# Adding y in step 1 of the last segments, and maxima of a block ahead of the wait for the last denominators

## The chip, the cores and the metric

The kernel runs on one core of a Trainium2 chip. The metric is the device time of one execution in microseconds (us). Five engines work side by side, each through its own program in order: TensorE (PE; its weight loads are listed apart as PEld), VectorE (DVE), ScalarE (ACT), GpSimd (POOL) and SyncE (SP, which here only issues DMAs). They wait for each other by semaphores.

## The reference

x is 2048 rows by 256, the context 1601 rows by 256. The reference is

- x = x + tanh(g_xattn) * (attention(layernorm(x), context) @ Wo + bo). The attention layer normalises its two inputs once more, has 16 heads of 64, clips the scaled scores to -11 and 11, and divides by the sum of the exponentials: softmax(clip(q k^T / 8)) v.
- x = x + tanh(g_ffn) * ffn(layernorm(x)). The feed-forward part (256 to 768 and back) has weights rounded to 4 bits in blocks of 32, and activations rounded to 16 bits by a scale of the whole tensor: `scale = max|x| / 32767`, so that no element of a stage can be rounded before the maximum of all of them is known. There are five such scales, one after the other.

Everything is float32.

## The kernel before

**Segments.** The attention runs over 32 segments (`SEGS`). A segment is a pair of heads and a block of 512 rows of x (`ORDER`): pair t // 4 and block t % 4 for t up to 23, then pairs 6 and 7, three blocks each, and in segments 30 and 31 block 3 of both. A segment has 13 steps (`ST`), each over 128 rows of the context. In a step

- TensorE computes the scores of two steps ahead (`scores`, L1080) into PSUM,
- ScalarE takes the exponential into `e_buf` (L509), and with that frees the scores' banks,
- VectorE clips it between exp(-11) and exp(11) (L793) and adds it to `acc`, the running sum for the denominators (`add_e`, L749), one step behind the clip,
- TensorE multiplies the clipped exponentials by the values (`values`, L1096).

**Jobs.** Two more PSUM banks (`ps_m`) are used in turn by jobs, whose order `segment_jobs` writes out for each segment; a job's number modulo 2 is its bank, and it waits (`bank_free`) until the job two before it has been taken out of the bank. TensorE does the jobs of a segment in step 0 (`at == st`), after the scores of step 2 and before the values of step 0. In their order they are: key and value projections for a later pair (`k`, `v`; only in the segments for which `kv_blocks` is not empty, 0 to 26), the next segment's q (L990), two halves of y for each segment in `y_segments` (L1039: the finished heads' output times Wo), the denominators of the segment or segments before (`den_job`, L1018: ones times `acc`), and in segments 27 to 29 three jobs that transpose quantised feed-forward weights (`wT`, L979). In segments 27 to 31 there is thus: q, 2 y, den, 3 wT in 27 and 29; q, 4 y, den, 3 wT in 28; q, 2 y, den in 30; and 2 y, den in 31.

ScalarE takes q out (L443), the denominators (`den_take`, L483) and the high parts of the transposed weights (L476), all after the exponential of step 2. VectorE takes y out: `add_y` (L785) adds a half of it to `xacc`. With `w_low` (L730) it takes the low parts of the weights. So in a segment without projections the chain in the two banks is: q is taken by ScalarE, then y half 1 can be written; y half 0 is taken by VectorE, then the denominators can be; y half 1 is taken, then the first `wT`; and so on.

**VectorE's order** is written out in its `run` (L788 to L822). In step 0 it clips and makes the last addition of the segment before; in step 1 it clips and joins the two halves of the segment before's output (`join_out`, L776); from step 2 on it clips and adds. In step 2 it then calls `add_y` for the segments that are due. In segments 29 to 31 `norm_piece` puts the layer norm for the feed-forward part in between: moments, small operations of a Newton iteration (`root_step`), and in segment 31 the maxima of the normalised rows of blocks 0 and 1 (`h_tops`, steps 1 and 2). ScalarE writes those rows (`h_normalise`, L488): eight after the exponential of step 0 of segment 31, four after that of step 12.

**The turn of the denominators.** SP moves them from one row to many partitions, VectorE inverts them in step 6 (L763), SP brings them back, and `scale_out` (L770) multiplies the output by them in step 11.

**The end of attention** (L824 to L852). TensorE multiplies segment 30's output by Wo (`y_last`, L1051), writes the denominators of segment 31 (`den_last`, L1027), waits for VectorE and multiplies the output of 31. VectorE joins the output halves, waits for the denominators, takes the maxima of block 2 (`h_tops(NBS - 2)`), inverts the denominators in two halves (L835), multiplies (L841), adds y (L846), and makes the layer norm of block 3. Behind it the first global scale is formed, the rows become integers, and the feed-forward matmuls begin (L1189).

Of the kernel before, what the change touches and what calls it, by code (L numbers as in the profile page):

```python
# [22 lines left out]
NBS = N // NB  # L23
# [58 lines left out]
def kv_blocks(t):  # L82

    if t < SEGS - 2 * NBS:
        return [(t // NBS + 1, t % NBS)] if t else [(1, 0)]
    return {WT0 - 3: [(PAIRS - 1, 0)], WT0 - 2: [(PAIRS - 1, 1)], WT0 - 1: [(PAIRS - 1, 2), (PAIRS - 1, 3)]}.get(t, [])
# [7 lines left out]
def turn_in(t):  # L94

    return next((i for i, segs in enumerate(DENS) if segs[-1] == t - 1), None)
# [6 lines left out]
def y_segments(t):  # L103

    if t <= WT0:
        return [t - 3] if t >= 3 else []
    return [t - 3, t - 2] if t == WT0 + 1 else [t - 2]
# [35 lines left out]
def bank_of(key):  # L143
    return JOBS[key] % 2


def place_of(key, seg):

    return JOBS[key] // 2


def attention_ffn(nc, x, ctx_rows, g_xattn, g_ffn, ln_l_w, ln_l_b, ln_c_w, ln_c_b,
                  Wq, Wkv, Wo, bo, w_gate, w_up, w_down, out):
    inv_rows = nc.dram_tensor("inv_rows", (4, NB), F32).ap()
    with ExitStack() as ctx:
# [102 lines left out]
        def await_job(eng, key, seg=None):  # L258

            eng.wait_ge(job_ready[bank_of(key)], place_of(key, seg) + 1)  # L260
# [339 lines left out]
        def _(dve):  # L600
# [40 lines left out]
            def top(dst, src):  # L641
                return dve.tensor_reduce(dst, src, AX_X, ALU.max, apply_absolute_value=True)  # L642
# [27 lines left out]
            def h_tops(b):  # L670

                dve.wait_ge(h_norm, 4 * b + 4)
                top(fst[:, 0, 2 * b:2 * b + 2],
                    z[:, 4 * b:4 * b + 4, :].rearrange("p (a t) d -> p a (t d)", a=2)).then_inc(h_top, 1)

            def norm_piece(t0, st, place):

                if (t0, st, place) in ((SEGS - 3, 4, 1), (SEGS - 2, 4, 1), (SEGS - 1, 3, 1)):
                    b = t0 - (SEGS - 3)
                    for half in range(2):  # L680
                        await_taken(dve, ("y", t0 - 2, half))
                    moments(LN3 + 4 * b, rows_of_block(b))
                k = 2 * (st - 5) + place
                if t0 == SEGS - 2 and 0 <= k <= 3 + 3 * NEWTON:
                    root_step(LN3, LN3 + 2 * NBS, k)
                k += 2
                if t0 == SEGS - 1 and 0 <= k <= 3 + 3 * NEWTON:
                    root_step(LN3 + 2 * NBS, LN3 + 3 * NBS, k)
                if t0 == SEGS - 1 and place == 1 and st in (1, 2):
                    h_tops(st - 1)  # L690
# [23 lines left out]
            def w_scales(w):  # L714

                blocks = wpiece[w].rearrange("p (n e) -> p n e", e=QB)
                dve.wait_ge(in_w, 64)
                link(top(wsc[:, w, 0, :], blocks))
                link(dve.tensor_scalar(wsc[:, w, 1, :], wsc[:, w, 0, :], 1.0 / WMAX, 1e-12, ALU.mult, ALU.max))
                dve.reciprocal(wsc[:, w, 2, :], wsc[:, w, 1, :]).then_inc(w_inverse, 1)  # L720

            def w_integers(w):
                dve.wait_ge(w_scaled, w + 1)
                dve.tensor_scalar(wpiece[w], wpiece[w], MAGIC, MAGIC, ALU.add, ALU.subtract).then_inc(w_round, 1)
# [8 lines left out]
            def w_multiply(w, row, ready, done):  # L733

                blocks = wpiece[w].rearrange("p (n e) -> p n e", e=QB)
                dve.wait_ge(ready, w + 1)
                dve.tensor_tensor(blocks, blocks, wsc[:, w, row, :].unsqueeze(2).to_broadcast([P, WBLK, QB]),
                                  ALU.mult).then_inc(done, 1)

            def add_e(seg, st):  # L740

                t0, r = seg.t0, rows_of(st)
                if st == 1:
                    a = e_buf[:, (ST * t0) % E_BUFS, :, :]
                else:
                    a = acc[0:r, t0 % 3, :, :]
                    dve.wait_ge(summed, seg.count(ST - 1, st - 1))
                dve.wait_ge(clip_done, seg.count(ST, st + 1))
                dve.tensor_tensor(acc[0:r, t0 % 3, :, :], a, e_buf[0:r, (ST * t0 + st) % E_BUFS, :, :],  # L749
                                  ALU.add).then_inc(summed, 1)  # L750

            def add_bias(b):

                dve.wait_ge(bias_scaled, 1)
                dve.wait_ge(lat_pool, NT - 4)
                rows = xacc[:, 4 * b:4 * b + 4, :]
                dve.tensor_tensor(rows, rows, bo_t[:, :].unsqueeze(1).to_broadcast([P, 4, DM]), ALU.add).then_inc(bias_added, 1)

            def invert_spread(i):

                dve.wait_ge(den_landed, 16 * rows_turned(i + 1))
                rows = 2 * QB * len(DENS[i])
                dve.reciprocal(inv_spread[0:rows, :], den_spread[0:rows, :]).then_inc(inv_done, 1)  # L763

            def scale_out(seg, t):

                i = turn_of(t)
                dve.wait_ge(inv_landed, 16 * rows_turned(i + 1))
                dve.wait_ge(o_out, Seg(t).count(1, 1))
                dve.tensor_tensor(oT[:, t % 3, :], oT[:, t % 3, :], rden[:, DENS[i].index(t), :], ALU.mult).then_inc(norm_done, 1)  # L770

            def join_out(seg, t):

                s = Seg(t)
                dve.wait_ge(o_half, s.count(1, 1))
                dve.tensor_tensor(oT[:, t % 3, :], ps_o[:, 1, :], oT[:, t % 3, :], ALU.add).then_inc(o_out, 1)  # L776

            def add_y(seg, t, half):
                key = ("y", t, half)
                n0 = 4 * ORDER[t][1] + 2 * half  # L780
                await_job(dve, key, seg)
                if t < NBS:
                    dve.wait_ge(bias_added, NBS)
                dst = xacc[:, n0:n0 + 2, :]
                dve.tensor_tensor(dst, ps_m[:, bank_of(key), :].rearrange("p (t d) -> p t d", d=DM), dst,  # L785
                                  ALU.add).then_inc(job_taken[bank_of(key)], 1)

            def run(seg):  # L788
                t0 = seg.t0
                for st in range(ST):  # L790
                    dve.wait_ge(exp_done, seg.count(ST, st + 1))
                    tile = e_buf[:, (ST * t0 + st) % E_BUFS, :, :]
                    dve.tensor_scalar(tile, tile, EXP_LO, EXP_HI, ALU.max, ALU.min).then_inc(clip_done, 1)  # L793
                    norm_piece(t0, st, 0)
                    if st >= 2:
                        add_e(seg, st - 1)
                    elif st == 0 and t0 >= 1:
                        add_e(Seg(t0 - 1), ST - 1)
                    elif t0 >= 1:
                        join_out(seg, t0 - 1)  # L800
                    if t0 == 0 and 4 <= st < 4 + NBS:
                        add_bias(st - 4)
                    if st == 6 and turn_in(t0) is not None:
                        invert_spread(turn_in(t0))
                    if st == 11 and turn_in(t0) is not None:
                        for t in DENS[turn_in(t0)]:
                            scale_out(seg, t)
                    if st == 2 and WQ0 <= t0 < WQ0 + 12 and (t0 - WQ0) % 2 == 0:
                        w = (t0 - WQ0) // 2
                        w_scales(w)  # L810
                        w_multiply(w, 2, w_inverse, w_scaled)
                    if st == 2:
                        for t in y_segments(t0):
                            add_y(seg, t, 0)
                            add_y(seg, t, 1)
                    if st == 2 and WQ0 <= t0 < WQ0 + 12 and (t0 - WQ0) % 2 == 0:
                        w_integers(w)
                        w_multiply(w, 1, w_round, w_quant)
                    if st == 2 and WT0 <= t0 < WT0 + 3:
                        for j in range(3):  # L820
                            w_low(t0 - WT0, j)
                    norm_piece(t0, st, 1)  # L822

            segments(dve, run)  # L824
            end = Seg(SEGS)
            t = SEGS - 1
            add_e(Seg(t), ST - 1)
            join_out(end, t)
            den_bank, w = bank_of(("den", t)), NB // 2
            await_job(dve, ("den", t))  # L830
            dve.wait_ge(o_out, SEGS)
            h_tops(NBS - 2)
            for half in range(2):
                part = slice(w * half, w * half + w)
                ins = dve.reciprocal(rden[:, 0, part], ps_m[:, den_bank, part])  # L835
# [440 lines left out]
```

## Time and profile before

| | us |
|---|---|
| median of 3 runs | 1190.52 |
| lowest and highest run | 1189.46, 1191.87 |
| the profiled execution | 1192.05 |
| its span, first to last instruction | 1190.1 |
| TensorE busy | 1094.1 |
| VectorE busy | 974.3 |
| ScalarE busy | 621.2 |

The profile is of one execution. The attention takes its first 1011 us, with some 29 us for each segment, the feed-forward part the rest. In the order of time, what stands in brackets is how long the engine was idle before the instruction, and whose work it then waited for. Matmuls of float32 are recorded in more than one piece, and neighbouring records overlap, because the ends of matmuls are modelled. [...]

### The profile page before, as it was taken

The page shows a single profiled execution, that of the slowest core. Times are in us where ns is not written, and L with a number is a line of the kernel's source. Part 1 is how long each engine was busy: PE and PEld are TensorE (multiplying, and loading weights), DVE is VectorE, ACT ScalarE, POOL GpSimd, SP SyncE. Part 2 cuts the span into 40 slices and gives each one's busy share as a digit, 9 for nine tenths or more (in the row PEclk, how much of TensorE's full clock was granted, in tenths as well). Part 3 has the DMA queues.
Part 4 walks back from the last instruction along what each step waited for, and adds up shares of the span by engine and source line. Part 5 has one row for each costly group of instructions (what it writes and reads, how often), then busy time and mean ns, then how long its engine had stood idle before and what let it go on. Part 6 is the DMA issues. An engine that isn't in the chain of part 4 may idle for free.

```text
span 1190.1 us, 20382 instructions
## 1 busy us (share of the span) xinstructions
PE 1094.1 (92%) x8424; PEld 497.5 (42%) x8424; DVE 974.3 (82%) x1319; ACT 621.2 (52%) x719; POOL 29.5 (2%) x41
## 2 busy tenths in 40 slices
PE   3999999999999999999999999999999989699039
PEld 2443344434443444344434443444333322587039
DVE  7467978797879788988898889887888898849986
ACT  2455555555555555555555555555555554449652
POOL 1200000000000000000000000000000000003200
PEclk9999999999999999999999999999999999799559
DMA  5000300010001000100010001000000000000002
GB/s 166 1 1 2 116 1 20 1 37 2 20 1 37 1 19 2 36 1 20 1 37 2 19 1 37 1 19 1 19 10 11 10 10 10 1 1 1 0 1 72
DMA packets 27324, 22.23 MB, mean 19 GB/s; under 512 B 8478, under 2 KB 23007, under 8 KB 27231
## 3 DMA queue, kind: packets, MB, share of 16 engines
q1 hardware_dynamic: 27230, 20.92, 5.8%
q8 instruction: 67, 1.10, 0.4%
q14 instruction: 27, 0.21, 0.1%
HBM read 18.55 MB, written 2.22 MB: 17 GB/s over the span
## 4 chain that ended last, share of the span: by engine, by line
PE 77%; DVE 12%; ACT 5%; issue 4%; DMA 1%; SPq 0%; POOL 0%; POOLq 0%; DVEq 0%; ACTq 0%
PE ps L1096 26%; PE ps L1080 26%; PE ps L990 4%; DVE acc L749 4%; PE ps L998 4%; PE ps L1039 4%; PE ps L1007 4%; PE ps L1189 3%; PE ps L1225 3%; DVE e_buf L793 3%; PE ps L1018 2%; ACT e_buf L509 1%; PE ps L979 1%; DVE gt L917 1%; ACT z L579 1%
## 5 line engine op out<-in xcount | busy, mean ns | idle before, releaser
L509 ACT ACTIVATE e_buf<-ps 128x1024 f32<-128x1024 f32 x416 | 426.1, 1025 | 312.3 <-PE ps L1080 312.3
L1096 PE MATMUL ps<-e_buf,vb 64*64 64x512 f32 x3328 | 436.3, 594 | 4.0 <-DVE e_buf L793 3.8
L749 DVE TENSOR_TENSOR acc<-acc,e_buf 128x1024 f32<-128x1024 f32 (+1 forms) x352 | 426.9, 1213 | 0.0
L793 DVE TENSOR_SCALAR e_buf<-e_buf 128x1024 f32<-128x1024 f32 x416 | 283.0, 680 | 108.5 <-ACT e_buf L509 108.3
L1096 PEld LDWEIGHTS ps<-e_buf,vb 64*64 64x64 f32 x3328 | 119.9, 133 | 243.4 <-issue 212.2
L1080 PE MATMUL ps<-qb,kb_even 64*64 64x512 f32 x1664 | 215.9, 589 | 1.3 <-ACT e_buf L509 1.3
L1080 PE MATMUL ps<-qb,kb_odd 64*64 64x512 f32 x1664 | 216.0, 589 | 0.0
L1080 PEld LDWEIGHTS ps<-qb,kb_odd 64*64 64x64 f32 x1664 | 63.8, 133 | 115.3 <-issue 115.3
L1080 PEld LDWEIGHTS ps<-qb,kb_even 64*64 64x64 f32 x1664 | 63.6, 133 | 115.3 <-issue 113.6
L785 DVE TENSOR_TENSOR xacc<-ps,xacc 128x512 f32<-128x512 f32 x60 | 40.9, 688 | 51.8 <-PE ps L1039 51.8
L1189 PE MATMUL ps<-hT,wgu 128*128 128x512 f32 x288 | 70.2, 407 | 2.3 <-DVE hT L886 2.3
L990 PE MATMUL ps<-latT,wst 128*128 128x512 f32 x128 | 63.1, 616 | 2.5 <-ACT latT L437 1.1
L1189 PEld LDWEIGHTS ps<-hT,wgu 128*128 128x128 f32 x288 | 55.9, 195 | 16.0 <-DVE hT L886 2.5
L1039 PE MATMUL ps<-wo_g,oT 128*128 128x256 f32 x240 | 59.1, 389 | 0.3 <-DVE xacc L785 0.3
L642 DVE TENSOR_REDUCE fst<-gt 128x2 f32<-128x1024 f32 x36 | 43.5, 1211 | 18.7 <-ACT gt L564 18.7
L1007 PEld LDWEIGHTS ps<-wst,ctxT 128*128 128x128 f32 (+1 forms) x416 | 49.4, 187 | 11.6 <-issue 11.2
L1039 PEld LDWEIGHTS ps<-wo_g,oT 128*128 128x128 f32 x240 | 43.1, 189 | 24.1 <-issue 14.2
L998 PE MATMUL ps<-ctxT,wst 128*128 128x512 f32 (+1 forms) x128 | 51.9, 532 | 0.0
L1007 PE MATMUL ps<-wst,ctxT 128*128 128x128 f32 (+1 forms) x416 | 51.3, 275 | 0.3 <-ACT vb L454 0.3
L1182 PE MATMUL ps<-ident,fsc 128*128 128x128 f32 x10 | 2.8, 399 | 46.6 <-DVE fsc L642 46.6
L443 ACT COPY qb<-ps 128x512 f32<-128x512 f32 x32 | 18.7, 586 | 44.4 <-PE ps L990 44.4
L749 DVE TENSOR_TENSOR acc<-e_buf 128x1024 f32<-128x1024 f32 x32 | 38.8, 1213 | 0.0
(118 smaller groups left out, 620.1 us busy)
## 6 DMA issues: line engine op xcount, KB each, us to landing
rden<-inv_rows SPq DMA_DIRECT2D x62, 128.0 KB, 2.8
xacc<-in_x_dram SPq DMA_DIRECT2D x4, 512.0 KB, 8.2
wst<-in_L_xattn_Wkv_dram SPq DMA_DIRECT2D x16, 128.0 KB, 2.6
out_dram<-z SPq DMA_DIRECT2D x7, 256.0 KB, 2.2
e_buf<-in_ctx_dram SPq DMA_DIRECT2D x3, 512.0 KB, 4.6
wst<-in_L_xattn_Wq_dram SPq DMA_DIRECT2D x8, 128.0 KB, 2.7
wo_raw<-in_L_xattn_Wo_dram SPq DMA_DIRECT2D x8, 128.0 KB, 3.3
den_spread<-den_row SPq DMA_DIRECT2D x62, 2.0 KB, 1.7
```

Source lines behind the costliest of these rows:

```text
L509: nc.scalar.activation(e_buf[:, g % E_BUFS, :, :], sc[:, g % 2, :, :], ACT.Exp, scale=float(DH) ** -0.5).then_inc(exp_done, 1)
L642: return dve.tensor_reduce(dst, src, AX_X, ALU.max, apply_absolute_value=True)
L749: dve.tensor_tensor(acc[0:r, t0 % 3, :, :], a, e_buf[0:r, (ST * t0 + st) % E_BUFS, :, :], ALU.add).then_inc(summed, 1)
L785: dve.tensor_tensor(dst, ps_m[:, bank_of(key), :].rearrange("p (t d) -> p t d", d=DM), dst, ALU.add).then_inc(job_taken[bank_of(key)], 1)
L793: dve.tensor_scalar(tile, tile, EXP_LO, EXP_HI, ALU.max, ALU.min).then_inc(clip_done, 1)
L990: ins = pe.matmul(bank, wst[:, at[0], 0, k, :], latT[:, k, b * NB:(b + 1) * NB], start=(k == 0), stop=(k == KT - 1))
L998: ins = pe.matmul(bank[:, 0:w], wst[:, at[0], 1, k, :], ctxT[:, k, b * NB:b * NB + w], start=(k == 0), stop=(k == KT - 1))
L1007: ins = pe.matmul(bank[0:r, P * i:P * i + P], ctxT[:, k, P * st:P * st + r], wst[:, at[0], 2, k, :], start=(k == 0), stop=(k == KT - 1))
L1039: ins = pe.matmul(bank[:, DM * m:DM * m + DM], oT[:, t % 3, n0:n0 + P], wo_g[:, p % 2, :], start=True, stop=True)
L1080: ins = pe.matmul(sc[at:at + DH, g % 2, h, :], kb[p % 2][rows, P * st + at:P * st + at + DH], qb[rows, t0 % 2, :], start=True, stop=True)
L1096: ins = pe.matmul(ps_o[DH * h:DH * h + DH, half, :], vb[rows, p % 2, st, DH * h:DH * h + DH], e_buf[rows, g % E_BUFS, h, :], start=(st == ...
L1189: ins = pe.matmul(out_ap, lhs(i), rhs(j), start=(first and n == 0), stop=(last and n == 2))
```

## The change

Two places in VectorE's program. In segments for which `kv_blocks` is empty (27 to 31), `add_y` is called in step 1, behind `join_out` and ahead of what `norm_piece` does there, instead of in step 2; in segments 3 to 26 it stays in step 2. At the end, `h_tops` of block 2 is called before VectorE waits for the last denominators.

```diff
@@ run of VectorE @@
                         w_scales(w)
                         w_multiply(w, 2, w_inverse, w_scaled)
-                    if st == 2:
+                    if st == (2 if kv_blocks(t0) else 1):
                         for t in y_segments(t0):
                             add_y(seg, t, 0)
                             add_y(seg, t, 1)
@@ after the segments @@
             join_out(end, t)
             den_bank, w = bank_of(("den", t)), NB // 2
+            h_tops(NBS - 2)
             await_job(dve, ("den", t))
             dve.wait_ge(o_out, SEGS)
-            h_tops(NBS - 2)
             for half in range(2):
```

## Rows read from the trace of the kernel before

**Rows 1.** The page, busy time of each engine in us.
```profile
PE 1094.1 (92%) x8424; PEld 497.5 (42%) x8424; DVE 974.3 (82%) x1319; ACT 621.2 (52%) x719; POOL 29.5 (2%) x41
```

**Rows 2.** Order of time, TensorE, segment 27: start, duration (us), engine, line, what.
```profile
852.30 1.97 PE L1039 MATMUL ps<-wo_g,oT 128*128 128x256 f32 x8
...
855.01 1.05 PE L1018 MATMUL ps<-acc,ones 128*32 128x512 f32 x4 [0.74 <-DVE xacc L785]
```

**Rows 3.** Order of time, ScalarE and VectorE, segment 27.
```profile
852.50 0.59 ACT L443 COPY qb<-ps 128x512 f32<-128x512 f32 x1 [0.86 <-PE ps L990]
852.55 0.67 DVE L793 TENSOR_SCALAR e_buf<-e_buf 128x1024 f32<-128x1024 f32 x1
...
853.15 1.21 DVE L749 TENSOR_TENSOR acc<-e_buf 128x1024 f32<-128x1024 f32 x1
854.28 1.27 DVE L785 TENSOR_TENSOR xacc<-ps,xacc 128x512 f32<-128x512 f32 x2
...
857.30 1.51 DVE L730 TENSOR_TENSOR wgu<-ps,wgu 128x512 fp32r<-128x512 f32 x2 [1.75 <-ACT wgu L476]
...
861.77 0.69 DVE L793 TENSOR_SCALAR e_buf<-e_buf 128x1024 f32<-128x1024 f32 x1 [1.65 <-ACT e_buf L509]
```

**Rows 4.** Order of time, TensorE and VectorE, segment 28.
```profile
885.25 2.00 PE L1039 MATMUL ps<-wo_g,oT 128*128 128x256 f32 x8 [0.29 <-DVE xacc L785]
886.42 0.69 DVE L785 TENSOR_TENSOR xacc<-ps,xacc 128x512 f32<-128x512 f32 x1 [0.63 <-PE ps L1039]
...
887.29 0.69 DVE L785 TENSOR_TENSOR xacc<-ps,xacc 128x512 f32<-128x512 f32 x1 [0.17 <-PE ps L1039]
...
889.47 0.69 DVE L730 TENSOR_TENSOR wgu<-ps,wgu 128x512 fp32r<-128x512 f32 x1 [1.49 <-ACT wgu L476]
```

**Rows 5.** Order of time, TensorE, segment 29.
```profile
917.42 1.05 PE L1018 MATMUL ps<-acc,ones 128*32 128x512 f32 x4 [0.28 <-DVE xacc L785]
```

**Rows 6.** Order of time, TensorE and VectorE, segment 30.
```profile
949.52 1.05 PE L1018 MATMUL ps<-acc,ones 128*32 128x512 f32 x4 [0.74 <-DVE xacc L785]
...
953.58 0.69 DVE L793 TENSOR_SCALAR e_buf<-e_buf 128x1024 f32<-128x1024 f32 x1 [3.51 <-ACT e_buf L509]
```

**Rows 7.** Order of time, VectorE, segment 31.
```profile
978.30 1.21 DVE L642 TENSOR_REDUCE fst<-z 128x2 f32<-128x1024 f32 x1
979.43 0.68 DVE L793 TENSOR_SCALAR e_buf<-e_buf 128x1024 f32<-128x1024 f32 x1
...
981.16 1.28 DVE L785 TENSOR_TENSOR xacc<-ps,xacc 128x512 f32<-128x512 f32 x2
982.36 1.21 DVE L642 TENSOR_REDUCE fst<-z 128x2 f32<-128x1024 f32 x1
987.54 0.69 DVE L793 TENSOR_SCALAR e_buf<-e_buf 128x1024 f32<-128x1024 f32 x1 [3.97 <-ACT e_buf L509]
```

**Rows 8.** Order of time, TensorE, segment 31.
```profile
975.37 1.99 PE L1039 MATMUL ps<-wo_g,oT 128*128 128x256 f32 x8
981.90 1.92 PE L1018 MATMUL ps<-acc,ones 128*32 128x512 f32 x4 [4.53 <-DVE xacc L785]
```

**Rows 9.** Stretches: length, busy (x instructions) of PE, PEld, DVE, ACT, POOL, PEclk, DMA.
```profile
981.90:984.90 3.00, 3.00 (x12) 0.73 (x16) 1.67 (x2) 0.58 (x1) 0.00 (x0) 0.50 0.00 0
990.00:1009.00 19.00, 16.68 (x139) 4.51 (x132) 18.90 (x41) 10.50 (x13) 0.00 (x0) 1.00 0.04 15
1030.80:1036.40 5.60, 5.60 (x13) 4.44 (x14) 4.97 (x8) 4.70 (x10) 0.00 (x0) 0.50 0.01 1
1036.50:1042.10 5.60, 5.60 (x26) 4.51 (x25) 2.44 (x2) 2.22 (x5) 0.00 (x0) 1.00 0.01 3
```

**Rows 10.** Order of time, ScalarE and VectorE, end of attention.
```profile
1004.31 2.06 ACT L488 ACTIVATE z<-xacc,lnt 128x256 f32<-128x256 f32 x4
...
1011.48 1.22 DVE L642 TENSOR_REDUCE fst<-z 128x2 f32<-128x1024 f32 x1 [1.14 <-PE ps L1027]
```

**Rows 11.** Order of time, TensorE, last values of segment 31.
```profile
1007.41 1.09 PE L1096 MATMUL ps<-e_buf,vb 64*64 64x512 f32 x8 [1.25 <-DVE e_buf L793]
```

## The prediction

> **What bounds the kernel now.** I read the page first. TensorE is busy for 92% of the span, VectorE for 82% [rows 1]. So a gain has to be time that TensorE spends waiting, or time in which VectorE alone sets the end. Then I read the order of time around the places that the diff touches: step 2 of segments 27 to 31 (the only ones for which `kv_blocks` is empty and `y_segments` is not), and the end of attention. In each of them the denominators' matmuls (L1018) stand in TensorE's program behind the two halves of y (L1039) and need the PSUM bank that VectorE's `add_y` (L785) frees. VectorE comes to `add_y` only after the clip and the addition of step 2, so TensorE stands: 0.74 us in segment 27 [rows 2], 0.28 in 29 and 0.74 in 30 [rows 5, 6]. In 28, which has two segments' y, it waits 0.29 before the second [rows 4]. In segment 31 it waits 4.53 us [rows 8]. At the end VectorE idles 1.14 us for the last denominators and takes the maxima of block 2 only afterwards [rows 10].
>
> **The change, part by part.** No operation is added or removed, and no DMA; only VectorE's order changes. What an operation of VectorE costs is read from one start to the next: a clip 0.60 us (852.55 to 853.15), an addition of e 1.13 (853.15 to 854.28) [rows 3], a half of y 0.60 (981.16 to 982.36 for two) and a maximum over a block 1.13 (978.30 to 979.43) [rows 7]. The queues of SP and GpSimd are moved past nothing: SP sends the denominators on when ScalarE has copied them, which comes earlier with them, and GpSimd's gate product waits for y of a pair long gone.
>
> *Segment 27.* VectorE is free at 852.55, where the clip of step 2 stands [rows 3]. The first half of y starts on TensorE at 852.30 [rows 2]. A half takes 1.17 us until VectorE can add it (885.25 to 886.42 [rows 4]), so `add_y` of half 0 runs from 853.47. Its bank is free 0.74 us after its start (981.16 to 981.90 [rows 7, 8]), at 854.21. TensorE ends both halves at 852.30 + 1.97 = 854.27, so the denominators start at 854.27 instead of 855.01: 0.74 us. The second half waits for ScalarE's copy of q, which comes at 852.50 by ScalarE's own order [rows 3] and doesn't move. Now what is queued behind: `add_y` of half 1 starts at about 854.32, then clip (+0.60), addition (+0.60) and the first `w_low` (+1.13), which is at 856.65. It started at 857.30 before, set by ScalarE; 0.74 us earlier is 856.56. So 0.09 is given back, since the third transposition waits for `w_low`. Net 0.65.
> *Segment 28.* TensorE ends the first y at 885.25 - 0.29 = 884.97 [rows 4] and began it 1.97 earlier, at 883.00. Half 0 is then added from 884.17, and its bank is free at 884.91, before TensorE asks for it. The 0.29 us wait goes, the rest of the chain to the denominators keeps its length (0.28 stays of it), and `w_low` comes 0.14 later than it could: the last add starts at 887.29 - 0.28 = 887.01, plus 2.33 is 889.34, against 889.47 - 0.28 = 889.19 [rows 4]. Net 0.14.
> *Segment 29.* It is built as 27; the wait is only 0.28 [rows 5], and with `w_low` giving back 0.08 the net is 0.20.
> *Segment 30.* No weights are transposed here, so the whole 0.74 stays [rows 6]. VectorE then idled 3.51 us before the clip of step 3, which covers the clip and addition that are now late.
> Sum of 27 to 30: 1.73. They add up, since in each segment the clip of step 3 waits for ScalarE's exponentials, and these for TensorE (1.65 us of idle in 27 [rows 3], 3.51 in 30), and everything behind it keeps its distances.
>
> *Segment 31.* Here y was ready at 975.37 + 1.99 = 977.36 [rows 8], long before VectorE came. The two halves come to 978.30, where the maximum of block 0 now stands, and 978.90, in place of 981.16 and 981.76 [rows 7]. The denominators start 0.74 after the first, at 979.04 instead of 981.90: 2.86 us, which is certain as far as VectorE's order goes. [...] The exponentials then allow the clip at 979.04 + 4.06 = 983.10. VectorE's own list (two halves, maximum of block 0, clip, addition, maximum of block 1, so 978.30 + 0.60 + 0.60 + 1.13 + 0.60 + 1.13 + 1.13) is through at 983.49, and that is the later one. So clip 3 moves from 987.54 to 983.49: 4.05 us, and VectorE's idle time of 3.97 there is used up. From then to the segment's end VectorE is busy for 18.90 of 19 us, while TensorE is for 16.68 [rows 9] and waits for its clips [rows 11], so the 4.05 reach the end. Lower end 2.86, if the clock falls all the same.
> [...]
>
> *The end.* The maxima of block 2 need `h_norm` of 12, given by ScalarE's four rows at 1004.31 + 2.06 = 1006.37 [rows 10], before VectorE joins the output halves. They move to 1011.48 - 1.14 = 1010.34, into the 1.14 us in which VectorE waits. The reciprocal then starts at 1011.48 instead of one maximum later, just as the denominators are ready. Gain 1.14; nothing runs beside VectorE on that path, so all of it counts. A lower bound is 0 if the reciprocal were held by something unseen; I see nothing that could.
>
> **Sum.** 1.73 + 4.05 + 1.14 = 6.92 us. The profiled execution took 1192.05 us (span 1190.1), which gives 1185.1. It is 1.53 above the median of the three runs, 1190.52, and a little above their highest, so I take the sum off the median: 1183.6. About 0.2% (2.4 us) is what a measurement of this kernel tells from no change.
>
> **Rivals.**
> *A. The clock falls in segment 31 all the same.* Then its gain is 2.86, the total 5.7 and the time 1184.8. For it: TensorE stands in that stretch for 1.67 us and then soon waits for VectorE again. Against: the granted clock stayed at 1.00 through the waits of 990 to 1009, 2.32 us in all [rows 9]. Chance 0.14.
> *B. The clock behind the attention is better.* [...] TensorE's wait at 1011 is 1.14 us shorter, and its work of before lies elsewhere in time; the low stretch may be shorter. Up to 2.8 us more: 1180.8 to 1183. Chance 0.14.
> *C. The new wait sets the pace.* In step 1 VectorE stands 0.92 us for half 0 and about 0.25 for half 1 in segments 27 to 30, with the clips behind it. If its idle time afterwards were less than 1.17, this came on top each time: 4 x 1.17 = 4.7, and the 1.73 would be lost, so the total is 5.19 - 4.7 = 0.5 and the time 1190.0. [...] Against it: [rows 3, 6] show 1.75 + 1.65 us of idle time behind it in segment 27 and 3.51 in 30. Chance 0.05.
> *D. Slower.* One mechanism is large enough: the clock at the first gate matmuls (L1189, from 1030.8). [...] For it: the low level starts from idle times that now lie elsewhere. Against: it was back at 1.00 after 5.6 us there, and within 5 us of matmuls in segment 31 [rows 9]. Chance 0.02.
> That the change doesn't do what it says would be that step 1's additions never free TensorE earlier; only if y came late in all five segments, which [rows 2, 4 to 8] exclude. Left for this and for the unforeseen, 1185.3 to 1188: 0.03.
>
> **Numbers.** My forecast, 1183.6, has 0.62. The range goes to 1181.0, which takes in most of B, and to 1187.2: A with the runs' own spread of 1.3 us about the median, and some 1 us of the terms of 27 to 30. Faster by over 0.2% is all but C and D: 0.93; within 0.2%: 0.05; slower: 0.02.
>
> **What would show it.** In the changed profile: L1018 starts right at the end of L1039 in segments 27 to 30 and with at most 1.7 us of idle time in 31; the granted clock is 1.00 all through segment 31; VectorE has no idle time before the clip of step 3 of segment 31; its wait on L1027 is gone; the waits of L785 for L1039 grow by about 4 us. Wrong would be: a 0.50 stretch in segment 31 (A), clips of step 3 without idle time before them in 27 to 30 (C), or a longer L1189 pass (B, D).

## The result, and the profile of the changed kernel

The changed kernel takes 1183.15 us (median of 6 runs, 1181.53 to 1185.2), the kernel before 1190.73 (6 runs): 7.6 us less. The ratio is 0.993, with a 95% interval of 0.992 to 0.9941, so by the ratio 8.3 us less (7.0 to 9.5). The forecast was 1183.6 in a range of 1181.0 to 1187.2. The profiled execution took 1181.53 us, its span 1179.7; that of before 1192.05 and 1190.1.

TensorE's order of time in the changed kernel, segments 27, 28, 30 and 31 and the end of attention (start, duration in us, line, what; in brackets the idle time before it):

```profile
850.51 1.97 PE L1039 MATMUL ps<-wo_g,oT 128*128 128x256 f32 x8
852.41 1.05 PE L1018 MATMUL ps<-acc,ones 128*32 128x512 f32 x4
...
880.55 3.88 PE L1039 MATMUL ps<-wo_g,oT 128*128 128x256 f32 x16
884.36 1.05 PE L1018 MATMUL ps<-acc,ones 128*32 128x512 f32 x4
...
945.83 1.05 PE L1018 MATMUL ps<-acc,ones 128*32 128x512 f32 x4
...
971.68 1.99 PE L1039 MATMUL ps<-wo_g,oT 128*128 128x256 f32 x8
975.35 1.05 PE L1018 MATMUL ps<-acc,ones 128*32 128x512 f32 x4 [1.67 <-DVE xacc L785]
...
1002.60 1.08 PE L1027 MATMUL ps<-acc,ones 128*64 128x512 f32 x4
```

The waits of [rows 2, 4, 5, 6] are gone (in segment 29 the denominators start at 914.40, 1.90 us after y at 912.50, where it was 2.25): in segment 28 the four halves of y are one row of 16 without a gap. The wait of 4.53 us [rows 8] is 1.67. VectorE's order of time, segments 27, 30 and 31 and the end:

```profile
851.58 0.69 DVE L785 TENSOR_TENSOR xacc<-ps,xacc 128x512 f32<-128x512 f32 x1 [0.74 <-PE ps L1039]
852.52 0.69 DVE L785 TENSOR_TENSOR xacc<-ps,xacc 128x512 f32<-128x512 f32 x1 [0.25 <-PE ps L1039]
853.13 0.68 DVE L793 TENSOR_SCALAR e_buf<-e_buf 128x1024 f32<-128x1024 f32 x1
853.73 1.22 DVE L749 TENSOR_TENSOR acc<-e_buf 128x1024 f32<-128x1024 f32 x1
854.86 1.35 DVE L730 TENSOR_TENSOR wgu<-ps,wgu 128x512 fp32r<-128x512 f32 x2
...
859.32 0.69 DVE L793 TENSOR_SCALAR e_buf<-e_buf 128x1024 f32<-128x1024 f32 x1 [1.65 <-ACT e_buf L509]
...
949.88 0.69 DVE L793 TENSOR_SCALAR e_buf<-e_buf 128x1024 f32<-128x1024 f32 x1 [1.52 <-ACT e_buf L509]
...
974.61 1.28 DVE L785 TENSOR_TENSOR xacc<-ps,xacc 128x512 f32<-128x512 f32 x2
975.81 1.21 DVE L642 TENSOR_REDUCE fst<-z 128x2 f32<-128x1024 f32 x1
976.93 0.68 DVE L793 TENSOR_SCALAR e_buf<-e_buf 128x1024 f32<-128x1024 f32 x1
977.53 1.22 DVE L749 TENSOR_TENSOR acc<-e_buf 128x1024 f32<-128x1024 f32 x1
978.66 1.22 DVE L642 TENSOR_REDUCE fst<-z 128x2 f32<-128x1024 f32 x1
979.79 0.69 DVE L793 TENSOR_SCALAR e_buf<-e_buf 128x1024 f32<-128x1024 f32 x1
...
1002.51 1.21 DVE L642 TENSOR_REDUCE fst<-z 128x2 f32<-128x1024 f32 x1
1003.73 1.76 DVE L835 RECIPROCAL rden<-ps 128x256 f32<-128x256 f32 x1
```

The new waits stand in step 1 (0.74 and 0.25 us), and behind them clip, addition and `w_low` (854.86) follow without a break. The clip of step 3 waits for ScalarE 1.65 us in segment 27, as before [rows 3], and 1.52 instead of 3.51 in segment 30 [rows 6]. In segment 31 that idle time (3.97 [rows 7]) is gone. Over all segments VectorE's waits of L785 for L1039 grew from 51.8 to 56.4 us, by the 4 us or so that the prediction named as a sign. At the end the reciprocal follows the maxima directly, 1.13 us after L1027; before it was 1012.62 - 1010.35 = 2.27, by these rows of the kernel before:

```profile
1010.35 1.08 PE L1027 MATMUL ps<-acc,ones 128*64 128x512 f32 x4
1012.62 1.75 DVE L835 RECIPROCAL rden<-ps 128x256 f32<-128x256 f32 x1
```

The stretches of the changed kernel (length, then the busy us of PE, PEld, DVE, ACT and POOL with their number of instructions, the clock granted to TensorE as a share of its full speed, PEclk in [rows 9], the busy share of the DMA engines and what they moved in GB/s) show no low clock from y of segment 31 to the first reciprocal, and the matmuls of L1189 begin again at 0.50, for some 3 us in this execution where it was 5.6 [rows 9].

```profile
972.00:1004.00 32.00, 27.31 (x208) 8.97 (x206) 31.10 (x56) 16.14 (x20) 0.00 (x0) 1.00 0.04 9
1021.90:1024.90 3.00, 2.97 (x7) 2.40 (x8) 3.00 (x5) 2.97 (x6) 0.00 (x0) 0.50 0.01 3
1025.20:1028.20 3.00, 3.00 (x15) 2.41 (x14) 2.75 (x4) 2.30 (x5) 0.00 (x0) 1.00 0.00 0
```

**Where the time went.** The two executions, cut at the same instructions. A row is the distance from its mark to the next.

| from | before | changed | less | forecast |
|---|---|---|---|---|
| start to y of 27 | 852.30 | 850.51 | 1.79 | 0 |
| y of 27 to y of 28 | 30.70 | 30.04 | 0.66 | 0.65 |
| y of 28 to y of 29 | 32.17 | 31.95 | 0.22 | 0.14 |
| y of 29 to y of 30 | 31.64 | 31.43 | 0.21 | 0.20 |
| y of 30 to y of 31 | 28.56 | 27.75 | 0.81 | 0.74 |
| y of 31 to L1027 | 34.98 | 30.92 | 4.06 | 4.05 |
| L1027 to reciprocal | 2.27 | 1.13 | 1.14 | 1.14 |
| reciprocal to L1189 | 18.18 | 18.20 | -0.02 | 0 |
| L1189 to the end | 159.30 | 157.77 | 1.53 | 0 |
| sum | 1190.10 | 1179.70 | 10.40 | 6.92 |

The six rows that the change touches give 7.10 us. The first row can't be the change's, which begins behind it. It and the last vary between executions: the profile of before has a stretch of 0.50 near its start, that of the changed kernel hasn't. A second profile of the changed kernel (below) had one, began y of 27 at 852.28, had the same middle rows within 0.01 us, and a last row of 159.77; its span, 1183.5, is 6.6 under that of before.

### The profile page after: what moved, and what is told of

The parts are those of the page before. It is cut to its first block, busy times and chain, and to the rows that moved or that the text cites. A ratio compares the mean times of both kernels' runs of the same rounds, so it can differ in the third digit from the quotient of the medians.

```text
span 1179.7 us, 20382 instructions
## 1 busy us (share of the span) xinstructions
PE 1088.9 (92%) x8424; PEld 495.7 (42%) x8424; DVE 974.4 (83%) x1319; ACT 621.4 (53%) x719; POOL 29.5 (3%) x41
## 4 chain that ended last, share of the span: by engine, by line
PE 83%; DVE 8%; ACT 4%; issue 4%; DMA 1%; POOL 0%; POOLq 0%; SPq 0%; DVEq 0%; ACTq 0%
PE ps L1096 29%; PE ps L1080 28%; PE ps L990 5%; PE ps L1039 4%; PE ps L998 4%; PE ps L1007 4%; PE ps L1189 3%; PE ps L1225 3%; DVE acc L749 2%; PE ps L1018 1%; DVE gt L917 1%; ACT z L579 1%; ACT z L581 1%; PE ps L979 1%; DVE fst L642 1%
## 5 line engine op out<-in xcount | busy, mean ns | idle before, releaser
L785 DVE TENSOR_TENSOR xacc<-ps,xacc 128x512 f32<-128x512 f32 x60 | 41.4, 691 | 56.4 <-PE ps L1039 56.4
L1189 PE MATMUL ps<-hT,wgu 128*128 128x512 f32 x288 | 69.0, 402 | 2.2 <-DVE hT L886 2.2
L990 PE MATMUL ps<-latT,wst 128*128 128x512 f32 x128 | 61.4, 602 | 2.5 <-ACT latT L437 1.2
L1189 PEld LDWEIGHTS ps<-hT,wgu 128*128 128x128 f32 x288 | 55.0, 192 | 15.7 <-DVE hT L886 2.5
L1039 PE MATMUL ps<-wo_g,oT 128*128 128x256 f32 x240 | 59.1, 390 | 0.0
L1039 PEld LDWEIGHTS ps<-wo_g,oT 128*128 128x128 f32 x240 | 43.0, 189 | 23.8 <-issue 14.2
```

The lines of the kernel that those rows point to most:

```text
L990: ins = pe.matmul(bank, wst[:, at[0], 0, k, :], latT[:, k, b * NB:(b + 1) * NB], start=(k == 0), stop=(k == KT - 1))
L1039: ins = pe.matmul(bank[:, DM * m:DM * m + DM], oT[:, t % 3, n0:n0 + P], wo_g[:, p % 2, :], start=True, stop=True)
L1189: ins = pe.matmul(out_ap, lhs(i), rhs(j), start=(first and n == 0), stop=(last and n == 2))
```

## The experiments

All times are medians; a difference in us is taken from the ratio to the kernel before on the same chip, with its interval. Since the clock matters, the table has also the time at 0.50: twice one less the mean granted clock, times the span, mean of the runs. This counts the clock as either 1.00 or 0.50, and in windows of 1 us over all 14 traces it is one of the two, or between them in the one window where it changes. The mean clock is on record to 0.001, which is 2.4 us of this time in one run, so differences of a few us mean something only over many runs. In each of the 14 traces some 51 us of it lie in one stretch of the feed-forward part (from about 1092 to 1105 us on), the same in all kernels. The kernels before have 72.9 us (beside the two parts apart, the segments and the first run of the maxima), 72.1 (beside y repeated, y behind the maxima and the first runs with matmuls ahead of L1189) and 73.9 (beside the runs marked as again and the matmuls at the end of attention); for the first row there is none.

| kernel | us | less than before | at 0.50 |
|---|---|---|---|
| both parts (the changed kernel) | 1183.15 | 8.3 (7.0 to 9.5) | 65.0 |
| the same, again | 1184.42 | 7.7 (5.7 to 9.9) | 67.4 |
| y in step 1 alone | 1185.94 | 5.8 (4.4 to 7.3) | 68.2 |
| of these, 31 alone | 1188.03 | 4.1 (2.9 to 5.4) | 69.1 |
| of these, 27 to 30 alone | 1189.78 | 2.0 (1.0 to 3.0) | 75.3 |
| the maxima alone | 1188.16 | 3.1 (2.0 to 4.1) | 68.2 |
| the maxima alone, again on another chip | 1188.69 | 3.1 (1.8 to 4.5) | 70.2 |
| before, y repeated in 31 | 1189.74 | 1.7 (0.5 to 3.0) | 70.3 |
| changed, y behind the maxima in 31 | 1184.19 | 6.8 (5.2 to 8.5) | 66.2 |
| before, matmuls added at the end of attention | 1190.67 | 1.3 (-0.1 to 2.7) | 66.8 |
| changed, matmuls added ahead of L1189 | 1182.19 | 9.2 (7.5 to 10.8) | 61.4 |
| changed, matmuls added at both places | 1180.27 | 10.8 (8.9 to 12.9) | 55.2 |
| the same, again on another chip | 1182.49 | 9.2 (6.9 to 11.4) | 59.8 |

### The two parts apart

Only the first hunk:

```diff
-                    if st == 2:
+                    if st == (2 if kv_blocks(t0) else 1):
```

> The kernel before with only the first part: y added in step 1 of segments 27 to 31. My theory (the parts are separate and each is a shortened wait): 7.58 us measured for the whole less 1.14 of the other part, so 6.0 to 6.5 us under the kernel before, with the maxima of block 2 again 1.14 us behind VectorE's wait for L1027. Rival (a fifth to a quarter of the gain comes from the clock behind the attention, rival B of the prediction, set off by the shorter wait at the end): more than 1.14 is lost, 2 us or more.

Measured: 1185.94 us, ratio 0.9951 (0.9939 to 0.9963), 5.8 us less (4.4 to 7.3). That is a little under the 6.0 to 6.5 expected, and the interval takes in both this and the rival's loss of 2 us or more, so it doesn't decide between them. The distances of segments 27 to 30 in its trace are those of the changed kernel. The trace showed something else at the end of segment 31, on TensorE:

```profile
997.12 1.09 PE L1096 MATMUL ps<-e_buf,vb 64*64 64x512 f32 x8 [0.72 <-DVE e_buf L793]
999.45 1.59 PE L1096 MATMUL ps<-e_buf,vb 64*64 64x512 f32 x8 [1.25 <-DVE e_buf L793]
1000.97 3.14 PE L1051 MATMUL ps<-wo_g,oT 128*128 128x256 f32 x8
```

The stretch of the same kernel behind them (the clock is the 0.53):

```profile
1000.50:1003.50 3.00, 3.00 (x10) 2.07 (x7) 1.87 (x3) 0.59 (x1) 0.00 (x0) 0.53 0.00 0
```

All 14 traces have these two waits ([rows 11] has the second). This time the clock fell after them: 32.56 us from y of 31 to L1027 instead of 30.92. It happened in 2 of the 7 traces in which the denominators of segment 31 had found it at 1.00 (this one and the one with matmuls ahead of L1189, 32.57 us).

Only the second hunk:

```diff
+            h_tops(NBS - 2)
             await_job(dve, ("den", t))
             dve.wait_ge(o_out, SEGS)
-            h_tops(NBS - 2)
```

> The kernel before with only the second part, the maxima of block 2 ahead of the wait. My theory: VectorE reaches its reciprocal 1.14 us earlier after the last denominators, the median falls by 1.1 us. [...]

> The maxima of block 2 moved alone, once more on another chip. If the 3 us stand: 2 to 3.5 us under the kernel before and some 4 to 5 us less at 0.50. If they were chance: 1.1 us.

Measured: 1188.16 and 1188.69 us, both with a ratio of 0.9974 (0.9966 to 0.9983, and 0.9962 to 0.9985), 3.1 us less. VectorE in the second trace:

```profile
1009.65 0.68 DVE L776 TENSOR_TENSOR oT<-ps,oT 128x512 f32<-128x512 f32 x1
1010.25 1.21 DVE L642 TENSOR_REDUCE fst<-z 128x2 f32<-128x1024 f32 x1
1011.47 1.76 DVE L835 RECIPROCAL rden<-ps 128x256 f32<-128x256 f32 x1
```

L1027 started at 1010.34 there: 1.13 us to the reciprocal, as forecast, so 1.14 of the 3.1 is VectorE's. The intervals (at least 1.8 us) exclude that it is all, so the 1.1 us of my theory missed and the size is that of rival B of the prediction, by which the clock does the rest (2 us or more). The time at 0.50 fell by 4.7 and 3.7 us, which points to the clock, and from L1189 to the end these two traces need 158.0 and 157.6 us, that of before 159.3; more on this below. But the parts together don't give the sum of the two alone (5.8 + 3.1 = 8.9 against 8.3 and 7.7, within the intervals).

### The first part, by segments

```diff
-                    if st == 2:
+                    if st == (1 if t0 == SEGS - 1 else 2):
```

> The kernel before with y added in step 1 of segment 31 alone. My theory: TensorE waits 1.67 us there instead of 4.53, its clock stays at 1.00, VectorE's idle time before the clip of step 3 is gone, and the median falls by 4.05 us. Rival A (the clock falls all the same): 2.9 us. Rival (VectorE's total work sets segment 31, so that an earlier add gains nothing): 0.

```diff
-                    if st == 2:
+                    if st == (1 if WT0 <= t0 < SEGS - 1 else 2):
```

> The kernel before with y added in step 1 of segments 27 to 30, not of 31. My theory: the shifts of 0.66, 0.21, 0.21 and 0.82 us that the changed kernel's trace shows add up to 1.9 us, and the wait of 4.53 us in segment 31 with its stretch at 0.50 is as before. Rival C (the waits of VectorE in step 1 come back later in the segment): within 0.5 us of the kernel before.

Measured: 4.1 us less for 31 alone (ratio 0.9966, 0.9955 to 0.9976), 2.0 for 27 to 30 (0.9983, 0.9975 to 0.9992). TensorE's denominators in segment 31 of the first:

```profile
980.04 1.05 PE L1018 MATMUL ps<-acc,ones 128*32 128x512 f32 x4 [1.67 <-DVE xacc L785]
```

The same of the second, 27 to 30 alone:

```profile
980.54 1.92 PE L1018 MATMUL ps<-acc,ones 128*32 128x512 f32 x4 [4.53 <-DVE xacc L785]
```

VectorE's clip of step 3 in the second:

```profile
987.09 0.69 DVE L793 TENSOR_SCALAR e_buf<-e_buf 128x1024 f32<-128x1024 f32 x1 [4.89 <-ACT e_buf L509]
```

The first kernel has 30.92 us from y of 31 to L1027, exactly the changed kernel's. The second has y of 27 to y of 31 in 121.17 us against 123.07, 1.90 less, and the long wait as before; in its trace the low clock behind it even lasted longer, clip 3 coming 6.55 us after the denominators; its runs' time at 0.50 is 75.3 us, over the 72.9 of the kernel before. The interval of 31 alone just reaches rival A's 2.9 us, but its trace, with the clock at 1.00, decides against it there. So both shares are where the table of distances has them, rival C (the waits of step 1 come back) falls, and so does the rival by which VectorE's total work sets segment 31.

### How much of segment 31 is the clock

```diff
-                for m in range(2):
+                for m in [0, 1] * (4 if t == SEGS - 3 and half else 1):
```

> The kernel before, where TensorE computes half 1 of y of segment 31 four times over instead of once (the same values into the same bank; the last time gives the signal), so that it works until about 980.2 us instead of 977.4 and waits 1.7 us instead of 4.5. VectorE's order is that of before. My theory (1.58 of the 4.05 us of segment 31 is the clock): the denominators start when they did, at 1.00 of the clock, the clip of step 3 follows 4.06 us after them instead of 5.64, and the median falls by 1.6 us although TensorE does more. Rival (the clock costs nothing there, all of the 4.05 is VectorE's order): the same as before.

```diff
+                    if t0 == SEGS - 1 and st == 1:
+                        for half in range(2):
+                            add_y(seg, t0 - 2, half)
```

This stands behind `norm_piece(t0, st, 1)` in the changed kernel's `run`, and the call ahead of it is left out for segment 31.

> The changed kernel, but in segment 31 the maxima of block 0 come first in step 1 and y is added behind them, 1.13 us later. My theory: TensorE then waits 2.80 us instead of 1.67, the exponentials of step 3 are ready 0.74 us after VectorE could clip them (1.13 less the slack of 0.39), so VectorE idles 0.74 us again and the time is 0.7 us over the changed kernel's if the clock stays at 1.00, 2.3 us over it where it falls. Rival (VectorE's list alone sets the clip, its order being of no matter): the changed kernel's time.

TensorE in the kernel before with y repeated:

```profile
973.34 4.58 PE L1039 MATMUL ps<-wo_g,oT 128*128 128x256 f32 x20
979.87 1.53 PE L1018 MATMUL ps<-acc,ones 128*32 128x512 f32 x4 [1.94 <-DVE xacc L785]
```

The stretch behind, in the same kernel:

```profile
980.40:983.60 3.20, 3.20 (x16) 0.80 (x16) 1.14 (x2) 0.59 (x1) 0.00 (x0) 0.50 0.03 6
```

TensorE in the changed kernel with y behind the maxima (its lines are 3 higher):

```profile
976.62 1.33 PE L1021 MATMUL ps<-acc,ones 128*32 128x512 f32 x4 [2.80 <-DVE xacc L785]
```

The stretch behind, in the same kernel:

```profile
977.30:980.50 3.20, 3.20 (x15) 0.80 (x17) 2.72 (x3) 0.59 (x1) 0.00 (x0) 0.50 0.01 1
```

And VectorE's clip of step 3 there:

```profile
982.32 0.69 DVE L793 TENSOR_SCALAR e_buf<-e_buf 128x1024 f32<-128x1024 f32 x1 [2.30 <-ACT e_buf L509]
```

The first expectation failed in its trace: the wait was down to 1.94 us, yet the clock fell, and clip 3 came at 985.57, 5.70 us after the denominators. In it nothing was gained: 35.05 us from y of 31 to L1027, where the kernel before has 34.98. Its runs are 1.7 us (0.5 to 3.0) faster by the ratio all the same, though only 0.6 by the medians, with 70.3 us at 0.50 against 72.1; that fits a clock that stays up in some of them, but no trace shows such a one. So this run does not show what the clock alone is worth. The second hit its worse case. The wait was 2.80 us, the clock fell, clip 3 came 5.70 us after the denominators and 10.50 after y of 31 began, where the changed kernel has 979.79 - 971.68 = 8.11: 2.39 us, against 2.3 expected. Against the changed kernel by the ratios it is 1.5 us slower, or 0.9 against its second measurement, with intervals that overlap.

Segment 30 has 953.58 - 949.52 = 4.06 us from the denominators to clip 3 [rows 6], segment 31 of the kernel before 987.54 - 981.90 = 5.64 [rows 7, 8]. The 1.58 between them goes with the clock: after the wait of 4.53 us it stood at 0.50 [rows 9], and the denominators' matmuls took 1.92 us where segment 30's took 1.05. Segment 31 itself gives the price too, since ScalarE's exponential of step 3 is there in every trace. These are the kernel before, the changed one, and the one with y behind the maxima:

```profile
986.48 1.02 ACT L509 ACTIVATE e_buf<-ps 128x1024 f32<-128x1024 f32 x1 [2.03 <-PE ps L1080]
978.34 1.02 ACT L509 ACTIVATE e_buf<-ps 128x1024 f32<-128x1024 f32 x1 [1.31 <-PE ps L1080]
981.26 1.02 ACT L509 ACTIVATE e_buf<-ps 128x1024 f32<-128x1024 f32 x1 [2.69 <-PE ps L1083]
```

It starts 986.48 - 981.90 = 4.58 us after the denominators in the first and 4.64 in the third, both with a stretch at 0.50, and 978.34 - 975.35 = 2.99 in the changed kernel, with the clock at 1.00, as in all 7 traces that wait 1.67 us. So the price is about 1.6 us, in kernels of different order (4.4 us after the denominators in two other traces with the long wait, 5.5 in that of 27 to 30 alone, where the stretch began earlier or lasted longer). Of the 4.05 us of the changed kernel 1.2 to 1.6 are this: VectorE's own list hides 0.39 of the 1.58 there (983.49 - 983.10 in the prediction). The length of the wait alone doesn't tell whether the price is paid: after 4.53 us the clock was low in all 5 traces that have this wait, after 1.67 in none of 7, after 1.94 and 2.80 in the one trace of each.

### The clock behind the attention

The kernel before, with matmuls whose result is not used where TensorE waits for the last denominators' inverse (bank 2 is free there):

```diff
+            def fill(bank, n):
+                for _ in range(n):
+                    pe.matmul(ps[:, bank, :], wgu[:, 0, 0, 0, 0:P], wgu[:, 0, 0, 0, 0:NB], start=True, stop=True)
             den_last()
+            fill(2, 14)
             y_last(SEGS - 1, 0)
```

> The kernel before, VectorE's order as it was, with 14 matmuls of no use behind the last denominators, so that TensorE waits some 0.5 us there instead of 3.45. The maxima moved alone gave 3.0 us on the mean of the spans where 1.14 is VectorE's, with 4.7 us less at 0.50 (two times one less the mean granted clock, times the span). If the rest comes from TensorE's shorter wait (rival B of the prediction), this kernel, in which nothing on VectorE moves, is 1 to 3 us under the kernel before and its time at 0.50 is 4 us or more under that of before. If the rest was chance among the runs: the kernel before's time, or 0.5 us under it for the last y at 1.00.

Measured: 1190.67 us, 1.3 less (-0.1 to 2.7), with 7 us less at 0.50. So less time at 0.50 doesn't by itself make the kernel faster by as much: in the 18.18 us from the reciprocal to L1189 in the trace of before, VectorE waits for TensorE only 0.56 us (the last y) and 0.58 (the matmul of the first scale). In its trace the clock was at 1.00 over the fill and the last y (1.13 us a half, where the second took 2.07), VectorE's wait of 0.56 us for it went (17.67 us from the reciprocal to L1189 instead of 18.18), and L1189 began at 0.50 like before:

```profile
1011.00:1016.00 5.00, 4.53 (x18) 3.14 (x18) 4.94 (x4) 0.00 (x0) 0.00 (x0) 1.00 0.00 0
1029.80:1035.40 5.60, 5.56 (x13) 4.40 (x14) 5.00 (x8) 4.69 (x10) 0.00 (x0) 0.50 0.01 1
```

This neither excludes nor shows that TensorE's shorter wait gives the maxima's extra 2 us.

The changed kernel, with matmuls ahead of L1189, and then also with 9 behind `den_last()`:

```diff
                 if j == KT * NBS - 1:
+                    fill(7, 3)
                     spread_max(0, 1, 0)
...
+            pe.wait_ge(h_int_a, 1)
+            fill(0, 8)
             half = FT * NBS
```

> The changed kernel with matmuls that compute nothing of use where TensorE waits between the attention and the first gate matmuls: 3 of 128x512 ahead of the first scale's matmul and 8 behind the last transposition, while the integers are made. If the stretch at 0.50 at the start of L1189 (3 us of it in the changed kernel's profile, 5.6 in that of before) follows from TensorE's idle time, the clock stays at 1.00 and 1.5 to 2.8 us are gained. If it doesn't, or if the added matmuls themselves hold up the first of L1189: 0, or up to 1.7 us lost.

> As the one before, with 9 more matmuls of no use behind the last denominators, where TensorE waits 2.32 us for VectorE. Expected on top: the second half of the last y runs at 1.00 (1.13 us instead of 2.07), VectorE's wait of 0.56 us for it goes, 0.5 us more. If the clock falls there for the later wait of 0.99 us too: nothing more.

> The changed kernel again, for comparison on the same chip: 7 to 8 us under the kernel before.

> The changed kernel with both groups of added matmuls, against the changed kernel on the same chip. If TensorE's idle time sets its clock behind the attention: 1.5 to 2.5 us under the changed kernel, with 8 to 10 us less at 0.50. If the gain of the first run was chance: the same as the changed kernel.

Measured: 1182.19 us with the first group, 1180.27 and 1182.49 with both; the changed kernel on the second of these chips 1184.42. Time at 0.50 falls from 65.0 and 67.4 us to 61.4, 55.2 and 59.8. In all three traces L1189 begins at 1.00. The second trace with both:

```profile
1020.90:1026.50 5.60, 5.60 (x24) 4.56 (x25) 5.35 (x9) 5.54 (x11) 0.00 (x0) 1.00 0.02 4
```

And in the changed kernel on the same chip:

```profile
1023.80:1029.40 5.60, 5.60 (x13) 4.38 (x14) 4.89 (x8) 4.70 (x10) 0.00 (x0) 0.50 0.00 1
```

24 matmuls instead of 13 in 5.6 us. In the kernel before, 13 ran at 0.50 where the next 5.6 us had 26 [rows 9], so half of 5.6, the 2.8 us of rival B, was lost there; here it isn't. With the first group alone part of it is lost again ahead of L1189: its last 8 added matmuls ran at 0.50 for 2.44 of their 3.23 us, where with both groups they took 2.11 and 2.12 us at 1.00, and L1189 started only when they were done, 19.30 us after the reciprocal instead of 18.20.

```profile
1021.46 3.23 PE L1179 MATMUL ps<-wgu 128*128 128x512 f32 x8
```

By the ratios it is 0.9 to 1.5 us under the changed kernel, less than the 1.5 to 2.8 expected and inside the intervals. The version with both groups is the fastest tried: 2 us under the changed kernel on the same chip by medians of 6 runs each (1.5 to 2.5 expected, with 8 to 10 us less at 0.50, where it is 7.6), but the intervals of the ratios (0.9904 to 0.9942 and 0.9917 to 0.9952) overlap, so that it beats the changed kernel is likely and not shown; that it beats the kernel before is.

All 14 traces together tell what the clock at L1189 is worth. From the start of L1189 on:

| traces | us at 0.50 | L1189 to the end |
|---|---|---|
| before; y repeated in 31; matmuls at the end of attention; y in step 1 alone; of these 31 alone | 5.6 to 6.1 | 159.3 to 159.9 |
| the changed kernel, again | 5.8 | 159.7 |
| the changed kernel, first; the maxima alone (two); y behind the maxima | 3.1 to 4.2 | 157.6 to 158.6 |
| y in step 1 of 27 to 30 alone | 3.1 | 157.9 |
| matmuls ahead of L1189 (three) | 0 | 156.6 to 156.9 |

Over the whole table each us at 0.50 costs about half a us of the time (156.6 to 156.9 us with none, 159.3 to 159.9 with 5.6 to 6.1). Of the five traces that have the maxima moved and no matmul added ahead of L1189, four have the shorter stretch; of the six that have neither, one has. This suggests that the maxima's extra 2 us are here, as rival B says. With one trace of a kernel and one of the five the other way it is not shown.

## Why the prediction was right

**Right, by its own steps.** Segments 27 and 29: 0.65 and 0.20 forecast, 0.66 and 0.21 found; the loss by `w_low` (0.09 forecast) is there too, as a wait of 0.82 us of the third transposition for VectorE, where it was 0.68. Segment 31: 4.05 against 4.06, the denominators after 1.67 us at a clock of 1.00, then VectorE's own list up to clip 3 with no idle time, as forecast. The 4.06 us that the forecast adds to 979.04 are segment 30's, 953.58 - 949.52 [rows 6]; that the clock stays at 1.00 after a wait of 1.67 us no trace of the kernel before shows (it shows it after 1.25 us [rows 9, 11]), and the 7 traces with that wait do. The end: 1.14 against 1.14. The experiments confirm that these are separate: 31 alone 4.1, 27 to 30 alone 2.0, and in segment 31 y behind the maxima instead of ahead of them costs 2.4 where the clock falls with it.

**Off in size.** *Segment 28* (0.14 forecast, 0.22 found) and *Segment 30* (0.74, 0.81). The step said that the denominators start at the end of the last y's row; they start 0.07 earlier, at 852.41 against 850.51 + 1.97 = 852.48, because the rows' ends are modelled and neighbouring rows overlap. In 27 and 29 the later `w_low` took the 0.07 back (0.14 in all). Sum of 27 to 30: 1.90 instead of 1.73.

**"nothing runs beside VectorE on that path, so all of it counts" was too little.** The second part alone measured 3.1 us twice, of which the step has 1.14. The rest goes with less time at 0.50, which rival B had for the whole change with a chance of 0.14. The traces point to the stretch at the start of L1189, but one trace for a kernel can't separate a habit from a draw, and why the shorter wait should shorten it stays open. For both parts together the excess over 7.1 is 0.5 us by medians and 1.2 by the first ratio, 0.6 by the second, inside their intervals. So the sum held for the path that it was made of; that the median came within half a us of it is in part luck, since the sum put the time from L1189 to the end as fixed, and it varies by 2 us between two traces of the changed kernel.

**Rival A** (the clock falls in segment 31 all the same) did not show at the denominators in 7 traces with the wait of 1.67 us, but the ground for its low chance was partly wrong. "The granted clock stayed at 1.00 through the waits of 990 to 1009" was one execution's luck: in 2 of the 7 traces it fell at their end. It costs 1.6 us when it does (32.56 and 32.57 us from y of 31 to L1027, where the changed kernel has 30.92). How long the clock is low differs between executions, then: the changed kernel had 3.1 us of L1189 at 0.50 in one trace and 5.8 in the other.

**Rival C** fell: the new waits in step 1 (0.99 us in segment 27) are covered, 1.65 and 1.52 us of idle time being left. **Rival D** did not occur: no run of the changed kernel took more than 1185.8 us. To lose the 6.9 us and 2.4 more would take 18.6 us more at 0.50, as half of such a stretch is lost (13 matmuls against 26 [rows 9]); the two traces of the changed kernel have 3.1 and 5.8 us at 0.50 at L1189, that of before 5.6.

## What to carry to other kernels

Two banks used in turn couple engines in the order of the jobs: ask for each consumer which producer waits for its bank, and place the consumer by that wait, even if it must then stand idle itself, as long as its idle time further on is larger (in segment 27 it stands 0.99 us and has 1.65 left). Where a short wait turns into a long one the clock may fall as well (after 1.67 us in none of 7 traces, after 4.53 in all 5), and 1.2 to 1.6 us of the 4.05 here were that. A gain that comes from the clock has to be measured over many runs, for one profile shows one draw (3.1 us at 0.50 at L1189 in one trace of the changed kernel, 5.8 in the other); and the mean granted clock beside the time doesn't give the gain alone, for 7 us less at 0.50 were worth 1.3 us where another engine set the time.

## What the runs showed of the hardware

- In one trace a wait of TensorE of 1.94 us came after 4.58 us of unbroken matmuls, and the clock was at 0.50 from about 0.5 us after matmuls resumed; after two waits of 0.72 and 1.25 us with work between them it fell in 2 traces and didn't in 5.
- The start of the kernel has such a stretch in some executions as well. y of 27 began between 849.98 and 850.66 us in the traces without it and between 852.02 and 853.54 in those with it, some 2 us that no change of this kind touches. In the two traces of the changed kernel this (1.77 us) and the time from L1189 to the end (1.93) are all but 0.1 of the 3.8 us between them.
- Matmuls added into TensorE's waits need not cost time: with 20 of them, 5.4 us of work in the second trace with both groups, the median was 1182.49 us against 1184.42 on the same chip, with intervals that overlap.
